# Two graph layers on one core: the last half chunk finished by blocks in PSUM, the first input chunk loaded alone, warming products of a constant zero

## Chip, core and metric

One core of one Trainium2 chip. The metric is the device time of one execution in microseconds (us); of the kernel before it is the median of 3 runs. TensorE is called PE here, VectorE DVE, ScalarE ACT, GpSimd POOL and SyncE SP, as in the profile.

## What is computed

With x (4096 x 128), adj (4096 x 4096) and small weights, all in float32:

```python
u, v = x, v_node_feats
for _ in range(3):
    v = mlp(adj @ u, uv_W1, uv_b1, uv_W2, uv_b2, uv_W3, uv_b3)   # leaky ReLU 0.01 after each layer
    u = mlp(adj @ v, vu_W1, vu_b1, vu_W2, vu_b2, vu_W3, vu_b3)
x = layernorm(x + v)
x = layernorm(x + adj @ (x @ gcn_W))
```

The second u of the last round is not used, so there are six products with adj: five of the rounds and the one of the last line. The kernel takes each product as adj @ (source @ W1): the source is multiplied by the first weight ahead of the product.

## The kernel before

**Tiles and visits.** The 4096 rows of adj are 8 chunks of 512. A tile is 1024 elements in each of 128 partitions: 512 rows of adj by 256 columns. Two tiles make a band, which one DMA of 1 MB loads (L530); `raw_of(t)` is where tile t lies. ACT makes the rounded copy `high` of a tile (`split` on ACT, L571), DVE the rest `low` (`split` on DVE, L728). A visit (`multiply`, L960) is six products of float32r: high with p_low and p_high (four, 512 columns each), then low with p_high (two). All work is put in program order by one counter n: at each n, each engine runs what is due there, and PE then runs visit n of 772. Each tile is split six visits ahead (`AHEAD`). A product's 8 sums are finished, or kept in `part`, and copied back into a PSUM bank by ACT (`seed`) when a later visit goes on with them.

**Start.** SP loads the first weight with x turned, in three pieces of 2, 2 and 4 chunks (`X_PIECES`), then four bands into `early`, then bands into the ring `raw`; a band of the ring is loaded again only after DVE has lowered both tiles that were in it (`load`, wait on `low_ready`). PE begins with 9 products of a zeroed block of `h` (`WARMING`, L975; DVE zeroes it, L724), which fill the time until x is there. Then `project_x` (L893) makes x @ uv_W1 for chunks 0 to 7, ACT raises each (L575) and DVE lowers it (L733). A float32 product of 128 columns is two records in the trace. `X_SPLIT` says before which tile's split a chunk is raised and lowered: chunks 0 to 3 before tile 0, and 4, 5, 6, 7 before tiles 2, 4, 6, 8. Tile t first needs chunk t // 2. The first sum's layer work begins at n = 16: ACT L623 and L624, DVE L754, then PE L866, L867, L869 at n = 19.

**End.** Sums of the last product become `chunks` with a start n: the visit after the sum closes, or 3 after the start before it, whichever is later (`SPACING`). The last row of adj is done apart (`last_sweep`): 12 tiles into a sum that is kept (ACT L589 copies it to `part`), then the 4 last tiles (`IN_HALVES`) are visited for rows 0 to 255 (half 0) and again for rows 256 to 511 (half 1), in products of 256 columns, each half in a bank of its own. For a half DVE adds sum and part (`finish_half`, L749, at the half's start), PE multiplies by gcn_W into `proj` (`project`, L900, start + 2), DVE adds x (L787), takes statistics (L791, L794; `measure`, start + 3), ACT takes the root (L656, start + 4), DVE inverts (L802, L805, start + 5), and ACT (half 0, L663, start + 6) or DVE (half 1, L811) normalizes. SP stores each half (L549). In `measure` of half 0 and `finish_half` of half 1, order on DVE is that of n; at the same n the chunk with the lower number comes first.

```python
HALF_PROJECT, HALF_MEASURE, HALF_ROOT, HALF_INVERT, HALF_NORMALIZE = 2, 3, 4, 5, 6
apart = SPACING[s.product] if s.product == self.sums[self.chunks[-1].total].product else BETWEEN
s.read = max(s.read, self.chunks[-1].start + apart)
```

In the kernel before, half 0 starts at n = 768 and half 1 at n = 772, after the last visit, 771; half 0's `project` is at n = 770 and its `measure` at n = 771.

Of the kernel before, what the change touches and what calls it, by code (L numbers as in the profile page):

```python
# [12 lines left out]
D = 128  # L13
# [23 lines left out]

X_PIECES = [2, 2, 4]

X_SPLIT = [0, 0, 0, 0, 2, 4, 6, 8]  # L40

CONSTS_AT, OTHER_CONSTS_AT, RESIDUAL_AT = 12, 22, 200

WARMING = 9

# [36 lines left out]
HALF = CHUNK // 2  # L82
IN_HALVES = 4
BETWEEN = 14


@dataclass
class Sum:


# [15 lines left out]
    seed: int = -1  # L106
    seeded: int = -1


# [18 lines left out]
class Plan:  # L128
# [100 lines left out]
    def last_sweep(self):  # L229
        rows = list(range(CHUNKS))[::-1]  # L230
        opened = [self.open(LAST, rows[r], "finish") for r in range(1, OPENED + 1)]
        for r in range(1, OPENED + 1):
            self.one(rows[r], self.band(rows[1:r + 1]), opened[r - 1])
        self.one(rows[0], self.band(rows[:1]), self.open(LAST, rows[0], "finish"))
        for r in range(1, OPENED + 1):
            self.one(rows[r], self.band(rows[:1]), opened[r - 1])
            self.one(rows[OPENED + r], self.band(rows[:OPENED + r + 1]), self.open(LAST, rows[OPENED + r], "finish"))
        columns = self.band(rows)
        self.one(rows[-1], columns[:-IN_HALVES], self.open(LAST, rows[-1], "keep"))
# [36 lines left out]
    def place_banks(self):  # L276

        holder = [None] * BANKS
        for i in sorted(range(len(self.sums)), key=lambda i: self.sums[i].opens):
            s = self.sums[i]  # L280
            s.bank = min(range(BANKS), key=lambda b: -1 if holder[b] is None else self.sums[holder[b]].read)
            if holder[s.bank] is not None:
                s.before = holder[s.bank]
                assert self.sums[s.before].read <= s.opens
# [17 lines left out]
def gnn_kernel(nc, adj, x_turned, x_nodes, constants, out):  # L302
# [4 lines left out]
    with ExitStack() as ctx:  # L307
# [58 lines left out]
        consts_set = sem("consts_set")  # L366
        nothing_set = sem("nothing_set")
        table_loaded = sem("table_loaded")
        band_loaded = [sem(f"band_loaded{i}") for i in range(EARLY + RAWS // IN_BAND + LATE)]
        high_ready = sem("high_ready")  # L370
# [6 lines left out]
        total_ready = sem("total_ready")  # L377
        half_ready = sem("half_ready")
        x_projected = sem("x_projected")
        first_raised = sem("first_raised")  # L380
# [133 lines left out]
        def _(sp):  # L514
# [8 lines left out]
            def load(t):  # L523
# [41 lines left out]
        def _(act):  # L565
            def split(t):
                buffer = buffers[t // IN_BAND]
                act.wait_ge(band_loaded[buffer], 16 * (len(loads_into(buffer, t // IN_BAND)) + 1))
                if t >= SLOTS:
# [13 lines left out]
            def keep(s):  # L583
# [74 lines left out]
            def normalize(i):  # L658
                act.wait_ge(shift_ready, i - NORM + 1)
                c = sum_of(i).chunk  # L660
                for j in blocks_in(i):
                    target = block_in(resid[:, blocks_of(c)] if normed(i) else part_of(c), j)
                    done = nc.scalar.activation(target, block_in(h[i % 2], j), ACT.Identity,  # L663
                                                bias=shift[:, j:j + 1], scale=rstd[:, j:j + 1])
# [12 lines left out]
            for n in range(END):  # L677
# [4 lines left out]
                for i, chunk in enumerate(chunks):  # L682
# [40 lines left out]
        def _(dve):  # L723
            nc.vector.memset(h[0][:, 0:D], 0.0).then_inc(nothing_set, 1)  # L724

            def split(t):
# [15 lines left out]
            def finish_half(i):  # L742
# [32 lines left out]
            def measure(i):  # L775
# [10 lines left out]
                columns = columns_in(chunks[i].half)  # L786
                nc.vector.tensor_tensor(h[i % 2][:, columns], source[:, columns],  # L787
                                        resid[:, blocks_of(sum_of(i).chunk)][:, columns], ALU.add).then_inc(x_added, 1)
                dve.wait_ge(x_added, i - NORM + 1)
# [18 lines left out]
            def normalize_half(i):  # L808

                for j in blocks_in(i):  # L810
                    done = nc.vector.tensor_scalar(block_in(part_of(sum_of(i).chunk), j), block_in(h[i % 2], j),  # L811
                                                   moments[:, j, 0:1], rstd[:, j:j + 1], op0=ALU.subtract, op1=ALU.mult)
# [49 lines left out]
        def _(pe):  # L862
# [34 lines left out]
            def turning(i, source, weight):  # L897

                for j in blocks_in(i):
                    done = nc.tensor.matmul(block_in(proj, j), block_in(source, j), weight, start=True,  # L900
# [18 lines left out]
            def project(i):  # L919
                if chunks[i].half < 0:  # L920
                    pe.wait_ge(total_ready, i - FINAL + 1)
                else:
                    pe.wait_ge(half_ready, chunks[i].half + 1)
# [18 lines left out]
            def multiply(n):  # L942
# [16 lines left out]
                def add(p, a, j, first, last):  # L959
                    return nc.tensor.matmul(bank[:, into], p[parity][:, block(j)], a[slot][:, columns(j)],  # L960
                                            start=(first and n == s.opens and s.seed < 0), stop=(last and n == s.closes),
                                            skip_group_check=s.seed >= 0)

# [8 lines left out]

            pe.wait_ge(nothing_set, 1)
            for _ in range(WARMING):
                nc.tensor.matmul(block_in(proj, 0), block_in(h[0], 0), block_in(h[0], 0), start=True, stop=True)  # L975
            for c in range(CHUNKS):
                project_x(c)
            for n in range(END):
                for i, chunk in enumerate(chunks):
                    if layered(i):  # L980
# [4 lines left out]
                        if n == chunk.turn:  # L985
                            turn(i)
                    elif n == place(i, PROJECT, HALF_PROJECT):
                        project(i)
                if n < len(visits):
                    multiply(n)  # L990
# [36 lines left out]
```

## Time and profile before

| | us |
|---|---|
| median of 3 runs (lowest, highest) | 1157.84 (1157.8, 1158.52) |
| the profiled execution's own time | 1157.88 |
| its span, first to last instruction | 1155.9 |
| PE busy | 1149.8 (99%) |
| ACT busy | 726.6 (63%) |
| DVE busy | 721.2 (62%) |
| float32r products L960, of 128x512 | mean 388 to 391 ns each |
| load of 1 MB into `raw`, issue to landing | 5.5 (median) |

The durations of products overlap, since each is pipelined behind the one before: what counts is the distance between their starts. The span leaves out 2.0 us of the profiled execution's time. The granted clock of the profile reads 1.00 of full in all stretches in which PE works.

### The profile page before, as it was taken

How to read it: one execution, taken by the hardware profiler on the slowest of the kernel's cores; microseconds unless marked ns; L12 is line 12 of the kernel's file. 1: busy time of each engine (PE TensorE's matmuls, PEld its weight loads, DVE VectorE, ACT ScalarE, POOL GpSimd, SP SyncE). 2: the span in 40 equal slices, each digit the busy share in tenths (PEclk: the TensorE clock that was granted, in tenths of full speed). 3: DMA queues.
4: the chain of work that ended last, by engine and by line, in shares of the span. 5: the costliest groups of instructions: out<-in, count | busy, mean ns of one | idle time of the engine just before them, and what ended most of it. 6: DMA issues, size and time to landing. Idle time of an engine off the chain costs nothing.

```text
span 1155.9 us, 14073 instructions
## 1 busy us (share of the span) xinstructions
PE 1149.8 (99%) x5314; PEld 961.3 (83%) x5314; DVE 721.2 (62%) x837; ACT 726.6 (63%) x925; POOL 4.2 (0%) x12
## 2 busy tenths in 40 slices
PE   9999999999999999999999999999999999999998
PEld 8888888888888888888888888888888888888887
DVE  6987545554665344765553585545558775459996
ACT  6876654455776444876554486544567874459884
POOL 0000000000000000000000000000000000000000
PEclk9999999999999999999999999999999999999999
DMA  9997656645855576666553584656558565579990
GB/s 384 387 365 274 231 197 244 229 178 195 319 185 207 190 276 234 242 231 255 218 182 145 196 349 182 224 197 234 198 196 327 206 230 191 216 274 371 373 382 22
DMA packets 39361, 281.42 MB, mean 243 GB/s; under 512 B 4416, under 2 KB 4800, under 8 KB 5632
## 3 DMA queue, kind: packets, MB, share of 16 engines
q1 hardware_dynamic: 38736, 278.69, 64.1%
q0 software_dynamic: 560, 1.84, 0.4%
q8 instruction: 44, 0.72, 0.2%
q14 instruction: 21, 0.17, 0.0%
HBM read 278.41 MB, written 2.10 MB: 243 GB/s over the span
## 4 chain that ended last, share of the span: by engine, by line
PE 99%; DVE 0%; issue 0%; ACT 0%; DVEq 0%
PE acc L960 90%; PE proj L900 4%; PE layer L869 1%; PE layer L866 1%; PE layer L867 1%; PE proj L975 0%; PE acc L893 0%; PE proj L893 0%; PE layer L893 0%; DVE stats L791 0%; DVE h L787 0%; DVE h L749 0%; DVE part L811 0%; ACT std L656 0%; DVEq L307 0%
## 5 line engine op out<-in xcount | busy, mean ns | idle before, releaser
L960 PE MATMUL acc<-high,p_low 128*128 128x512 f32 x1544 | 603.0, 391 | 0.0
L960 PE MATMUL acc<-high,p_high 128*128 128x512 f32 x1544 | 598.9, 388 | 0.0
L728 DVE TENSOR_TENSOR low<-raw,high 128x1024 fp32r<-128x1024 f32 x482 | 562.2, 1218 | 47.5 <-ACT high L571 46.8
L571 ACT ACTIVATE high<-raw 128x1024 fp32r<-128x1024 f32 x482 | 485.9, 1054 | 70.9 <-PE acc L960 49.0
L960 PE MATMUL acc<-low,p_high 128*128 128x512 f32 x1544 | 473.8, 388 | 0.0
L960 PEld LDWEIGHTS acc<-low,p_high 128*128 128x128 f32 x1544 | 289.1, 188 | 60.1 <-DVE low L728 0.5
L960 PEld LDWEIGHTS acc<-high,p_high 128*128 128x128 f32 x1544 | 290.1, 188 | 58.1
L960 PEld LDWEIGHTS acc<-high,p_low 128*128 128x128 f32 x1544 | 290.0, 188 | 57.8
L754 DVE TENSOR_TENSOR h_low<-h,h_high 128x512 fp32r<-128x512 f32 x40 | 27.6, 690 | 223.4 <-ACT h L624 223.4
L623 ACT ACTIVATE h_high<-acc,consts 128x512 fp32r<-128x512 f32 x40 | 27.5, 686 | 165.0 <-PE acc L960 165.0
L765 DVE TENSOR_TENSOR p_low<-proj,p_high 128x512 fp32r<-128x512 f32 x32 | 22.1, 690 | 64.1 <-ACT p_high L647 64.1
L759 DVE TENSOR_TENSOR h_low<-h,h_high 128x512 fp32r<-128x512 f32 x32 | 22.1, 692 | 54.1 <-ACT h L632 54.1
L630 ACT ACTIVATE h_high<-layer,consts 128x512 fp32r<-128x512 f32 x32 | 22.1, 689 | 41.6 <-PE layer L869 41.6
L637 ACT ACTIVATE h<-layer,consts 128x512 f32<-128x512 f32 x32 | 22.1, 690 | 40.5 <-PE layer L869 39.6
L647 ACT ACTIVATE p_high<-proj 128x512 fp32r<-128x512 f32 x32 | 19.2, 599 | 41.7 <-PE proj L900 41.7
L728 DVE TENSOR_TENSOR low<-late,high 128x1024 fp32r<-128x1024 f32 x32 | 36.9, 1216 | 0.0
L900 PEld LDWEIGHTS proj<-consts,h 128*128 128x128 f32 x256 | 33.5, 191 | 3.2 <-DVE h L749 0.8
L900 PE MATMUL proj<-consts,h 128*128 128x128 f32 x256 | 33.9, 275 | 0.6 <-DVE h L749 0.6
L632 ACT ACTIVATE h<-layer,consts 128x512 f32<-128x512 f32 x40 | 27.3, 683 | 8.9 <-PE layer L869 8.9
L571 ACT ACTIVATE high<-late 128x1024 fp32r<-128x1024 f32 x32 | 31.9, 1046 | 0.0
L589 ACT ACTIVATE part<-acc 128x512 f32<-128x512 f32 x36 | 21.4, 596 | 12.1 <-PE acc L960 10.9
L624 ACT ACTIVATE h<-acc,consts 128x512 f32<-128x512 f32 x40 | 27.3, 683 | 0.0
(60 smaller groups left out, 333.4 us busy)
## 6 DMA issues: line engine op xcount, KB each, us to landing
raw<-adj_dram SPq DMA_DIRECT2D x241, 1024.0 KB, 5.5
late<-adj_dram SPq DMA_DIRECT2D x16, 1024.0 KB, 7.4
early<-adj_dram SPq DMA_DIRECT2D x4, 1024.0 KB, 11.7
input<-x_dram SPq DMA_DIRECT2D x1, 2048.0 KB, 11.3
out_dram<-part POOLq DMA_DIRECT2D x7, 256.0 KB, 6.5
input<-x_turned_dram SPq DMA_DIRECT2D x1, 1024.0 KB, 6.9
input<-x_turned_dram SPq DMA_DIRECT2D x1, 576.0 KB, 4.1
input<-x_turned_dram SPq DMA_DIRECT2D x1, 512.0 KB, 4.9
```

What stands on the lines that cost most here:

```text
L571: nc.scalar.activation(high[t % SLOTS][:], raw_of(t), ACT.Copy).then_inc(high_ready, 1)
L623: nc.scalar.activation(h_high[:], summed(i)[:], ACT.Prelu, bias=bias, alpha=SLOPE).then_inc(first_raised, 1)
L624: nc.scalar.activation(h[i % 2][:], summed(i)[:], ACT.Prelu, bias=bias, alpha=SLOPE).then_inc(first_ready, 1)
L630: nc.scalar.activation(h_high[:], layer[0][:], ACT.Prelu, bias=bias, alpha=SLOPE).then_inc(second_raised, 1)
L632: nc.scalar.activation(h[i % 2][:], layer[0][:], ACT.Prelu, bias=bias, alpha=SLOPE).then_inc(second_ready, 1)
L637: nc.scalar.activation(h[i % 2][:], layer[1][:], ACT.Prelu, bias=b[f"{way_of(i)}_b3"], alpha=SLOPE).then_inc(third_ready, 1)
L728: nc.vector.tensor_tensor(low[t % SLOTS][:], raw_of(t), high[t % SLOTS][:].bitcast(F32), ALU.subtract).then_inc(low_ready, 1)
L754: nc.vector.tensor_tensor(h_low[:], h[i % 2][:], h_high[:].bitcast(F32), ALU.subtract).then_inc(first_lowered, 1)
L759: nc.vector.tensor_tensor(h_low[:], h[i % 2][:], h_high[:].bitcast(F32), ALU.subtract).then_inc(second_lowered, 1)
L765: nc.vector.tensor_tensor(p_low[k % 2][:, blocks_of(c)], proj[:], p_high[k % 2][:, blocks_of(c)].bitcast(F32), ALU.subtract).then_inc(p_lo ...
L900: done = nc.tensor.matmul(block_in(proj, j), block_in(source, j), weight, start=True, stop=True)
L960: return nc.tensor.matmul(bank[:, into], p[parity][:, block(j)], a[slot][:, columns(j)], start=(first and n == s.opens and s.seed < 0), st ...
```

## The change

At the start, x comes in pieces of 1, 1, 2 and 4 chunks, the first band is loaded by two DMAs of one tile each with a semaphore of its own for the first, the raising of chunks 4 to 7 moves from before tiles 2, 4, 6, 8 to before tiles 5, 7, 9, 11, and the warming products are 8 and read a constant zero that POOL writes before the engines start. At the end, two tiles are visited by halves in place of four. Half 1 goes on in the bank of the kept sum, so that only columns 0 to 255 are kept, and DVE copies its two blocks out one by one. The halves' residual is copied into PSUM by ACT beforehand (`seed_residuals`), block by block into layer[0], layer[0], layer[1] and proj; the products with gcn_W add to it there, and statistics and normalization read PSUM. There are 770 visits then; half 0 closes at n = 767 and starts at 768, half 1 closes at 769 and starts at 771.

```diff
-X_PIECES = [2, 2, 4]
-X_SPLIT = [0, 0, 0, 0, 2, 4, 6, 8]
+X_PIECES = [1, 1, 2, 4]
+X_SPLIT = [0, 0, 0, 0, 5, 7, 9, 11]
-WARMING = 9
+WARMING = 8
-IN_HALVES = 4
+IN_HALVES = 2
...
+            self.sums[total].continues = whole if half else -1
...
+            if s.continues >= 0:
+                s.bank = self.sums[s.continues].bank
...
-                sp.dma_start(band_in(buffer), adj[tiles[t][0], tiles[t][1] // IN_BAND]).then_inc(band_loaded[buffer], 16)
+                band = adj[tiles[t][0], tiles[t][1] // IN_BAND]
+                if t == 0:
+                    sp.dma_start(raw_of(0), band[:, 0:TILE]).then_inc(first_loaded, 16)
+                    sp.dma_start(raw_of(1), band[:, TILE:]).then_inc(band_loaded[buffer], 16)
+                else:
+                    sp.dma_start(band_in(buffer), band).then_inc(band_loaded[buffer], 16)
...
+            def shown(i):
+                if chunks[i].half < 0:
+                    return [h[i % 2]] * IN_CHUNK
+                return [layer[0], layer[0], layer[1], proj]
...
-                nc.scalar.activation(part_of(s.chunk), acc[s.bank][:], ACT.Copy).then_inc(part_kept, 1)
+                columns = columns_in(0 if (s.product, s.chunk) == (LAST, sum_of(len(chunks) - 1).chunk) else -1)
+                nc.scalar.activation(part_of(s.chunk)[:, columns], acc[s.bank][:, columns], ACT.Copy).then_inc(part_kept, 1)
+            def seed_residuals():
+                last = len(chunks) - 1
+                residual = resid[:, blocks_of(sum_of(last).chunk)]
+                act.wait_ge(second_ready, FINAL)
+                act.wait_ge(third_ready, NORM)
+                act.wait_ge(normed_ready, CHUNKS)
+                act.wait_ge(x_added, last - 1 - NORM)
+                nc.scalar.activation(layer[0][:, columns_in(0)], residual[:, columns_in(0)], ACT.Copy).then_inc(residual_seeded, 1)
+                for j in blocks_in(last):
+                    nc.scalar.activation(block_in(shown(last)[j], j), block_in(residual, j), ACT.Copy).then_inc(residual_seeded, 1)
...
+                        if n == chunk.start - 4 and chunk.half == 0:
+                            seed_residuals()
...
-            nc.vector.memset(h[0][:, 0:D], 0.0).then_inc(nothing_set, 1)
...
-                nc.vector.tensor_tensor(h[i % 2][:, columns], acc[s.bank][:, columns], part_of(s.chunk)[:, columns],
-                                        ALU.add).then_inc(half_ready, 1)
+                if s.half == 0:
+                    nc.vector.tensor_tensor(h[i % 2][:, columns], acc[s.bank][:, columns], part_of(s.chunk)[:, columns],
+                                            ALU.add).then_inc(half_ready, 1)
+                else:
+                    for j in blocks_in(i):
+                        nc.vector.tensor_copy(block_in(h[i % 2], j), block_in(acc[s.bank], j)).then_inc(half_ready, 1)
...
+                if chunks[i].half < 0:
+                    nc.vector.tensor_tensor(h[i % 2][:], source[:], resid[:, blocks_of(sum_of(i).chunk)],
+                                            ALU.add).then_inc(x_added, 1)
                 for j in blocks_in(i):
-                    nc.vector.bn_stats(stats[:, j, :], block_in(h[i % 2], j)).then_inc(stats_ready, 1)
+                    if chunks[i].half == 1:
+                        dve.wait_ge(proj_done, i + 1 + blocks_in(i).index(j))
+                    nc.vector.bn_stats(stats[:, j, :], block_in(shown(i)[j], j)).then_inc(stats_ready, 1)
...
+            def project_half(i):
+                half = chunks[i].half
+                pe.wait_ge(residual_seeded, 1 + 2 * half)
+                pe.wait_ge(half_ready, half + 1)
+                for nth, j in enumerate(blocks_in(i)):
+                    if half == 1:
+                        pe.wait_ge(half_ready, half + 1 + nth)
+                    done = nc.tensor.matmul(block_in(shown(i)[j], j), block_in(h[i % 2], j), w["gcn_W"], start=False,
+                                            stop=True, skip_group_check=True)
+                    if half == 1 or nth == 1:
+                        done.then_inc(proj_done, 1)
...
-            pe.wait_ge(nothing_set, 1)
+            zeros = nc.const_aps.tensor(0.0, [D, D], F32)
             for _ in range(WARMING):
-                nc.tensor.matmul(block_in(proj, 0), block_in(h[0], 0), block_in(h[0], 0), start=True, stop=True)
+                nc.tensor.matmul(block_in(proj, 0), zeros, zeros, start=True, stop=True)
```

The normalization of both halves (ACT L663, DVE L811) reads `shown(i)[j]` in place of `h`.

## Rows read from the trace of the kernel before

**Rows 1.** The page: the span, and the shares of the chain that ended last.

```profile
span 1155.9 us, 14073 instructions
...
PE 99%; DVE 0%; issue 0%; ACT 0%; DVEq 0%
```

**Rows 2.** Timeline of the start, 0 to 14: start, duration, engine, line, operation, [idle before].

```profile
0.74 1.33 SPq L517 DMA_DIRECT2D input<-x_turned_dram  x3
...
1.05 4.21 PE L975 MATMUL proj<-h 128*128 128x128 f32 x18 [1.05 <-DVE h L724]
...
5.06 1.78 PE L893 MATMUL proj<-input 128*128 128x128 f32 x8
...
6.68 1.95 PE L893 MATMUL layer<-input 128*128 128x128 f32 x16
...
12.85 0.47 PE L960 MATMUL acc<-high,p_low 128*128 128x512 f32 x1
```

**Rows 3.** DMA issues of the page: KB each, us from issue to landing.

```profile
input<-x_turned_dram SPq DMA_DIRECT2D x1, 1024.0 KB, 6.9
input<-x_turned_dram SPq DMA_DIRECT2D x1, 576.0 KB, 4.1
```

**Rows 4.** Timeline of ACT, 0 to 60: three splits that waited for a band.

```profile
11.02 2.00 ACT L571 ACTIVATE high<-early 128x1024 fp32r<-128x1024 f32 x2 [0.86 <-DMA early<-adj_dram]
...
19.24 2.01 ACT L571 ACTIVATE high<-early 128x1024 fp32r<-128x1024 f32 x2 [0.86 <-DMA early<-adj_dram]
...
35.30 2.01 ACT L571 ACTIVATE high<-raw 128x1024 fp32r<-128x1024 f32 x2 [1.56 <-DMA raw<-adj_dram]
```

**Rows 5.** Timeline of DVE, 10 to 60: splits, lowering of x, lowering of the first layer.

```profile
12.11 2.36 DVE L728 TENSOR_TENSOR low<-early,high 128x1024 fp32r<-128x1024 f32 x2 [1.23 <-ACT high L571]
...
22.99 0.68 DVE L733 TENSOR_TENSOR p_low<-proj,p_high 128x512 fp32r<-128x512 f32 x1
23.59 9.16 DVE L728 TENSOR_TENSOR low<-raw,high 128x1024 fp32r<-128x1024 f32 x8
...
38.49 0.69 DVE L754 TENSOR_TENSOR h_low<-h,h_high 128x512 fp32r<-128x512 f32 x1 [0.88 <-ACT h L624]
```

**Rows 6.** Timeline of PE and its weight loads, 20 to 42: tile 8's low, first layer.

```profile
24.86 0.30 PEld L960 LDWEIGHTS acc<-low,p_high 128*128 128x128 f32 x2 [0.29 <-DVE low L728]
...
39.50 0.39 PE L869 MATMUL layer<-h_low,w_high_uv_W 128*128 128x512 f32 x1
```

**Rows 7.** Timeline of SP, 27 to 29: the load of tiles 18 and 19.

```profile
28.24 0.33 SPq L530 DMA_DIRECT2D raw<-adj_dram  x1
```

**Rows 8.** Timeline of the end, 1140 to 1156, all engines.

```profile
1144.02 0.60 ACT L589 ACTIVATE part<-acc 128x512 f32<-128x512 f32 x1 [2.90 <-PE acc L960]
...
1148.13 0.61 PE L900 MATMUL proj<-consts,h 128*128 128x128 f32 x4
...
1148.49 0.36 PE L960 MATMUL acc<-high,p_low 128*128 128x256 f32 x1
...
1149.23 0.49 DVE L791 BATCH_NORM_STATS2 stats<-h 128x6 f32<-128x128 f32 x2
...
1149.64 0.30 DVE L794 BATCH_NORM_AGGREGATE moments<-stats 128x2 f32<-128x6 f32 x2
...
1149.77 0.40 PE L960 MATMUL acc<-low,p_high 128*128 128x256 f32 x2
...
1150.26 0.42 DVE L749 TENSOR_TENSOR h<-acc,part 128x256 f32<-128x256 f32 x1 [0.32 <-PE acc L960]
...
1150.74 0.71 PE L900 MATMUL proj<-consts,h 128*128 128x128 f32 x4 [0.57 <-DVE h L749]
...
1150.99 0.88 ACT L663 ACTIVATE part<-h,shift,rstd 128x128 f32<-128x128 f32 x2 [0.72 <-DVE shift L805]
...
1151.95 0.49 DVE L791 BATCH_NORM_STATS2 stats<-h 128x6 f32<-128x128 f32 x2
...
1153.22 0.60 DVE L811 TENSOR_SCALAR part<-h,moments,rstd 128x128 f32<-128x128 f32 x2
```

More of the change, by code:

```diff
@@ L107 @@
     seeded: int = -1
+    continues: int = -1
 @dataclass
@@ L238, in last_sweep @@
         columns = self.band(rows)
-        self.one(rows[-1], columns[:-IN_HALVES], self.open(LAST, rows[-1], "keep"))
+        whole = self.open(LAST, rows[-1], "keep")
+        self.one(rows[-1], columns[:-IN_HALVES], whole)
         last = [self.tile(rows[-1], column) for column in columns[-IN_HALVES:]]
@@ L366, in gnn_kernel @@
         consts_set = sem("consts_set")
-        nothing_set = sem("nothing_set")
         table_loaded = sem("table_loaded")
+        first_loaded = sem("first_loaded")
         band_loaded = [sem(f"band_loaded{i}") for i in range(EARLY + RAWS // IN_BAND + LATE)]
@@ L378, in gnn_kernel @@
         half_ready = sem("half_ready")
+        residual_seeded = sem("residual_seeded")
         x_projected = sem("x_projected")
@@ L567, in split @@
                 buffer = buffers[t // IN_BAND]
-                act.wait_ge(band_loaded[buffer], 16 * (len(loads_into(buffer, t // IN_BAND)) + 1))
+                if t == 0:
+                    act.wait_ge(first_loaded, 16)
+                else:
+                    act.wait_ge(band_loaded[buffer], 16 * (len(loads_into(buffer, t // IN_BAND)) + 1))
                 if t >= SLOTS:
@@ L662, in normalize @@
                     target = block_in(resid[:, blocks_of(c)] if normed(i) else part_of(c), j)
-                    done = nc.scalar.activation(target, block_in(h[i % 2], j), ACT.Identity,
+                    done = nc.scalar.activation(target, block_in(shown(i)[j], j), ACT.Identity,
                                                 bias=shift[:, j:j + 1], scale=rstd[:, j:j + 1])
@@ L785, in measure @@
                         dve.wait_ge(std_ready, i - NORM)
[L786 to L789, printed above, removed]
+                if chunks[i].half < 0:
+                    nc.vector.tensor_tensor(h[i % 2][:], source[:], resid[:, blocks_of(sum_of(i).chunk)],
+                                            ALU.add).then_inc(x_added, 1)
+                    dve.wait_ge(x_added, i - NORM + 1)
                 for j in blocks_in(i):
-                    nc.vector.bn_stats(stats[:, j, :], block_in(h[i % 2], j)).then_inc(stats_ready, 1)
+                    if chunks[i].half == 1:
+                        dve.wait_ge(proj_done, i + 1 + blocks_in(i).index(j))
+                    nc.vector.bn_stats(stats[:, j, :], block_in(shown(i)[j], j)).then_inc(stats_ready, 1)
                 for nth, j in enumerate(blocks_in(i)):
@@ L810, in normalize_half @@
                 for j in blocks_in(i):
-                    done = nc.vector.tensor_scalar(block_in(part_of(sum_of(i).chunk), j), block_in(h[i % 2], j),
+                    done = nc.vector.tensor_scalar(block_in(part_of(sum_of(i).chunk), j), block_in(shown(i)[j], j),
                                                    moments[:, j, 0:1], rstd[:, j:j + 1], op0=ALU.subtract, op1=ALU.mult)
@@ L897, in turning @@
             def turning(i, source, weight):
-                for j in blocks_in(i):
+                for j in range(IN_CHUNK):
                     done = nc.tensor.matmul(block_in(proj, j), block_in(source, j), weight, start=True,
@@ L919, in project @@
             def project(i):
[L920 to L923, printed above, removed]
+                pe.wait_ge(total_ready, i - FINAL + 1)
                 if i > FINAL:
@@ L960, in add @@
                     return nc.tensor.matmul(bank[:, into], p[parity][:, block(j)], a[slot][:, columns(j)],
-                                            start=(first and n == s.opens and s.seed < 0), stop=(last and n == s.closes),
-                                            skip_group_check=s.seed >= 0)
+                                            start=(first and n == s.opens and s.seed < 0 and s.continues < 0), stop=(last and n == s.closes),
+                                            skip_group_check=s.seed >= 0 or s.continues >= 0)
                 for j in range(PER_TILE):
@@ L986, in _ @@
                             turn(i)
-                    elif n == place(i, PROJECT, HALF_PROJECT):
+                    elif chunk.half < 0 and n == chunk.start + PROJECT:
                         project(i)
+                    elif chunk.half >= 0 and n == chunk.start + HALF_PROJECT:
+                        project_half(i)
                 if n < len(visits):
```

2 lines of the change are left out of this document (added).

## The prediction

> **What bounds the kernel now.** The page comes first: of the span of 1155.9 us, PE is 99% of the chain that ended last [rows 1]. No other engine can shorten the kernel between the first visit and the last; only what PE does before 12.85 us, waits inside its stream, and what follows its last visit can. The timeline of the start shows PE never idle from 1.05 on: 9 warming products (18 records, 0.22 us each), then the eight projections, then visit 0 at 12.85 [rows 2]. The first 8 records of projection last 0.20 each (5.06 to 6.68), the other 56 take 6.17 us, 0.110 each: the lower level of the clock (1.2 GHz), then the higher one (2.4 GHz) from about 6.5, though the granted clock reads 1.00 throughout. Behind PE, three chains run close: bands landing just in time for ACT [rows 4], DVE without a gap from 12.11 on [rows 5], and one place where PE waited for it, tile 8's `low` at 24.86, 0.29 us [rows 6]. At the end the last visit is used by DVE at 1150.26 and the last normalization ends at 1153.82, so 3.56 us of tail before the store [rows 8].
>
> The profiled execution took 1157.88 us, 0.04 above the median; the sum is made against it. What a measurement of this kernel can tell from no change is about 0.2%, 2.3 us; both ends of this change are smaller.
>
> **Start, warming and projections.** The wait for DVE's zeros goes, so PE can begin where SP does, at about 0.74 in place of 1.05; 16 records at 0.22 end at 4.3. The first piece of x is 320 KB in place of 576. It landed at 0.74 + 4.1 = 4.84; the last piece (1024 KB, issued about 1.6, 6.9 later) landed at 8.5 [rows 3], so 1536 KB took 3.7 us and 256 KB less are worth 0.6: landing at about 4.2. Projections begin at 4.3, not 5.06. If the clock rises at 6.5 as before, 10 records run at 0.22 and 54 at 0.110, and visit 0 comes at 12.45: 0.4 earlier. One SP issue more for x and one more for the band cost 0.4 us each on SP (three took 1.33), but the band behind them lands at 11.02, at the end of a queue that is never empty from the first piece on: nothing.
>
> **Start, the chain behind it.** PE keeps these 0.4 us only if `low` of the next tiles is earlier too. The first half band needs half of the 2.5 us between 8.5 and 11.02: ACT starts at 9.8, DVE lowers tile 0 at 10.9, tile 1 at 12.1 to 13.3. Then tile 2 needs the second band, at the same rate 2.5 after the first, at 13.5, so DVE idles till about 14.5; before, that hole held a chunk of x, which `X_SPLIT` now puts off. The fourth band lands at 19.24 in either kernel (the queue's bytes are the same), so DVE begins tile 6 at 20.3, against 20.7 before (two splits ahead of 22.99). From there DVE is saturated: a split each 1.14 us (9.16 for 8), a lowering of x each 0.61 (22.99 to 23.59) [rows 5]. Before, one lowering was left, and tile 8 was ready at 24.80. Now three are, before tiles 7, 9 and 11: tile 7 is ready at 20.3 + 1.14 + 0.61 + 1.21 = 23.3, tile 9 at 26.15, tile 11 at 20.3 + 5 x 1.14 + 3 x 0.61 + 1.21 = 29.05. Between tile 8's `low` at 24.99 and L869 at 39.50 lie 64 products, 0.227 each, so a visit is 1.36 [rows 6]. PE uses a late tile about 0.2 after it is ready (24.80 to 24.99: the weight load at 24.86 and 0.13 of it) and before it reached tile 11 at 24.99 + 3 x 1.36 = 29.07. Now it reaches it at 29.05 + 0.2 = 29.2. So the 0.4 is eaten at tiles 7, 9 and 11, and the start costs **+0.15**; bounds: -0.4 (the chain is a little faster than this) and +0.3.
>
> The loads of later bands are released by DVE's lowering. That of tiles 18 and 19 was issued at 28.24, behind tile 11 [rows 7]; now at 29.05, 0.8 later. It landed at 35.30, 7.1 us after issue, where the median is 5.5, so 1.5 us were queueing and much of the 0.8 disappears in it. What would be late next is the first layer: ACT's copies queue behind tiles 18 and 19, DVE's L754 ends at 39.18, PE uses it at 39.50 [rows 5, 6], a slack of 0.32. I take the landing as 0.3 later, so **0**; bounds 0 and +0.5 (0.8 less 0.3).
>
> **End, PE.** Two tiles, visited twice in 6 products of 256 columns, are visited once in 6 of 512: 24 records at 0.12 go, 12 at 0.227 come, 0.16 less. Half 0's projection leaves the middle of half 1's visits: between 1148.01, where the last record before it began, and 1148.49 lay 0.48 in place of 0.12 [rows 8]. **-0.52** together, by which the last visit ends earlier.
>
> **End, tail.** Both halves' projections now come after the last visit: half 0's is at n = 770, as far as PE gets when its visits are out. `measure` of half 0 is at n = 771 and so is `finish_half` of half 1, and half 0 has the lower number. DVE therefore waits for half 0's projection and takes its statistics before it copies out half 1. Let A be the moment at which DVE can use the last visit (1150.26 before, 0.37 after its last record began). Half 0's four records begin 0.12 behind that record and last 0.61 [rows 8], so statistics start at A + 0.40. The two aggregates begin 0.41 after that (1149.23 to 1149.64) and last 0.30 together; the next instruction can begin before they end, and I take 0.22 after their start, an estimate between 0.1 and 0.3. The copies start at A + 1.03. A copy of 128 columns: from 0.42 for 256 and 0.69 for 512 (a two-input add, the nearest row), 0.29; bounds 0.2 and 0.35. First copy out at A + 1.32, PE's first product 0.06 later, two records, 0.71 less 0.22 = 0.49: A + 1.87. The second block is 0.2 behind. Statistics, root and inverse follow as before: from the start of the first statistics to the end of normalization 1.87 us were taken (1151.95 to 1153.82, all in instructions that stay). The second statistics now starts at A + 2.1, its place before was 0.2 behind the first, so the end is A + 2.1 - 0.2 + 1.87 = A + 3.77. Half 0's normalization on ACT (0.88) starts after its inverse, at about A + 1.85, and ends at A + 2.75, just where the root of half 1 is wanted; 0.05 for that. A + 3.8 in place of A + 3.56: **+0.24**. In it are the two additions that go: half 0's residual add stood outside, half 1's 0.42 inside. They are seeded by ACT, three copies of at most 0.6 each near 1141, where ACT idled 2.90 [rows 8], and each later wait on them is long over. Half 1's first visit waits for ACT's copy of the kept half; that took 0.60 from 1144.02 and two visits of 0.72 lie between. Without that cover it would cost those 0.6.
>
> The row of L811, 0.60 for two normalizations of 128 columns out of SBUF, is kept for the same out of PSUM: x's lowering with a PSUM input and the first layer's with none take 0.68 and 0.69 [rows 5]. The Trainium skill (VectorE: DVE Perf Modes, "Why PSUM operands drop a tier") says that an operand in PSUM holds a float32 operation to one element a cycle, where one with a single input from SBUF may take two. No row before shows L811 from PSUM; by that rule the two would grow by half of 128 columns at 1.05 ns each, 0.07 apiece, and the sum by 0.13.
>
> **Sum.** 1157.88 + 0.15 + 0 - 0.52 + 0.24 = 1157.75; against the median **1157.7**.
>
> **Rivals.** (1) *The start keeps its gain*: the fourth band lands earlier, or ACT and DVE have slack that this sum does not see. For it: before, tile 6 was only just late. Against: DVE has no idle time in rows 5. Then -0.4 for +0.15: 1157.2. (2) *Slower*: the postponed lowerings delay the loads of tiles 18 to 23 in full, and PE waits at L869. It decides from a landing 0.32 us later than 35.30. Price 0.5: 1158.3, and with tail copies at their upper bound 1158.7. (3) *The clock*: if x's first piece lands late (at 4.8) behind shorter warming, PE idles about 0.5 us before the clock has risen, and the projections stay at the lower level: 54 records at 0.11 more, 5.9 us: 1163.6. Against it: PE was busy from 1.05 and would be but for that half microsecond. The Trainium skill (TensorE: Matmul & The Clock Gate, "What's actually happening") says that the gate's timing is not tied to the kernel's start; no single trace shows that. (4) *The change does not do what it says*: that half 1 is finished block by block can save 0.2 us at most, behind half 0's statistics; this is in the sum and has no chance of its own.
>
> **How the numbers follow.** Forecast 0.55 (own range 1157.3 to 1158.1), rival 1 0.25, rival 2 0.17, rival 3 0.03. 1156.9 to 1158.7 holds the forecast and rivals 1 and 2 with the bounds of the copies (0.2) and most of the spread of runs (0.7). Only rival 3 leaves the 0.2%: slower 0.03; faster 0.01; same 0.96.
>
> **What would show it.** Right: PE's first projection at 4.3, visit 0 at 12.4 to 12.5, new waits of PE's weight loads on DVE at tiles 7, 9 and 11, with tile 11's `low` used at 29.2; at the end four records of projection right behind the last visit, DVE's statistics of half 0 ahead of the copies, and 3.8 us from A to the last normalization. Wrong: visit 12 earlier than before by 0.3 (rival 1); a wait at L869 (rival 2); projection records at 0.22 after 7 us (rival 3); copies ahead of half 0's statistics.

## The result, and the profile after

| | before | after |
|---|---|---|
| median of 22 runs each (lowest, highest), us | 1157.89 (1157.67, 1158.52) | 1159.55 (1158.96, 1160.95) |
| profiled execution, its own time | 1157.88 | 1159.06 |
| its span | 1155.9 | 1157.3 |

The ratio after to before is 1.0015, interval [1.0009, 1.0021]: slower by 1.66 us, where 1157.7 was forecast and 1158.7 was the upper end of the range. It lies inside the 0.2% that the prediction called no change, and outside its range. The times also spread more than before (2.0 us against 0.9). One execution each of e2_band, e4_warm, e5_split, e7_134 and e11_116 below took 1279 to 6156 us; without it the median falls by at most 0.2, and as it was the profiled one of e5_split (6156) and of e7_134 (3052, PE slow throughout), nothing is read from the trace of the first and only the start of its DMA from that of the second.

The profiled execution lies near the fast edge of the 22, so its 1.18 us of difference (1.4 by the spans) shows the pattern and not the whole size.

First the timeline of the start of the changed kernel, to be held against [rows 2] (start, duration, engine, line, operation, [idle before]):

```profile
0.74 1.81 SPq L532 DMA_DIRECT2D input<-x_turned_dram  x4
...
0.78 3.37 PE L1027 MATMUL proj<-const-float32-0.0 128*128 128x128 f32 x16 [0.78 <-PEq L1058]
...
3.99 1.05 PE L935 MATMUL proj<-input 128*128 128x128 f32 x8
...
4.88 1.06 PE L935 MATMUL layer<-input 128*128 128x128 f32 x8
...
7.94 1.13 PE L935 MATMUL layer<-input 128*128 128x128 f32 x8 [2.00 <-DMA input<-x_turned_dram]
...
10.38 2.92 PE L935 MATMUL acc<-input 128*128 128x128 f32 x24 [0.42 <-DMA input<-x_turned_dram]
...
13.95 0.48 PE L1012 MATMUL acc<-high,p_low 128*128 128x512 f32 x1
```

The first projection starts 1.07 us sooner than before, and its records last 0.11 at once: in this execution the clock was at its higher level by 3.99. Then PE stands still for 2.00 us for chunk 2 and 0.42 for chunk 4, and visit 0 begins at 13.95, 1.10 later than before. In the profiled execution before nothing waited for x. Why x is late is in the DMA engines' rate over three stretches (length, granted clock, busy share, GB/s), first of the kernel before, then of the changed one:

```profile
3.00:5.00 2.00, 1.00 1.00 409
5.00:6.50 1.50, 1.00 1.05 442
6.50:8.00 1.50, 1.00 1.00 421
```

```profile
3.00:5.00 2.00, 1.00 1.03 340
5.00:6.50 1.50, 1.00 0.77 178
6.50:8.00 1.50, 1.00 1.04 401
```

From 5.0 to 6.5 the changed kernel moves 178 GB/s in place of 442: 0.27 MB against 0.66. With the 69 GB/s less before, 0.53 MB are missing by 6.5, 1.2 us of DMA at full rate, and all that is queued behind is late by that and more. ACT's splits, to be held against [rows 4], show it:

```profile
11.47 1.06 ACT L594 ACTIVATE high<-early 128x1024 fp32r<-128x1024 f32 x1 [0.88 <-DMA early<-adj_dram]
12.73 1.06 ACT L594 ACTIVATE high<-early 128x1024 fp32r<-128x1024 f32 x1 [0.20 <-DMA early<-adj_dram]
15.26 2.01 ACT L594 ACTIVATE high<-early 128x1024 fp32r<-128x1024 f32 x2 [1.47 <-DMA early<-adj_dram]
...
20.54 1.06 ACT L594 ACTIVATE high<-early 128x1024 fp32r<-128x1024 f32 x1 [0.35 <-DMA early<-adj_dram]
```

The half band that was to land at 9.8 landed at 11.47, the fourth band at 20.54 and not 19.24. Behind that come waits of PE's weight loads for DVE's `low`, five in place of two (before: 0.18 us at 21.99, tile 6, and 0.29 at 24.86, tile 8); three of them:

```profile
17.63 0.30 PEld L1012 LDWEIGHTS acc<-low,p_high 128*128 128x128 f32 x2 [0.20 <-DVE low L764]
...
24.67 0.30 PEld L1012 LDWEIGHTS acc<-low,p_high 128*128 128x128 f32 x2 [0.28 <-DVE low L764]
...
30.40 0.30 PEld L1012 LDWEIGHTS acc<-low,p_high 128*128 128x128 f32 x2 [0.28 <-DVE low L764]
```

They bring the 1.10 to 1.47 (chunk 1's turn into `proj` begins at 74.06, before at 72.59), and that stays until the end. Nothing is added at the first layer: tiles 18 and 19 land 0.97 later than before (35.30), but PE is 1.45 late by then, and its first-layer product L911 comes 1.46 after that of [rows 6]. The issue of that load, its split and the product:

```profile
30.38 0.33 SPq L550 DMA_DIRECT2D raw<-adj_dram  x1
...
36.27 2.01 ACT L594 ACTIVATE high<-raw 128x1024 fp32r<-128x1024 f32 x2 [0.62 <-DMA raw<-adj_dram]
...
40.96 0.39 PE L911 MATMUL layer<-h_low,w_high_uv_W 128*128 128x512 f32 x1
```

The end of the changed kernel, to be held against [rows 8]:

```profile
1150.63 0.40 PE L1012 MATMUL acc<-low,p_high 128*128 128x256 f32 x2
1150.88 0.61 PE L977 MATMUL layer<-consts,h 128*128 128x128 f32 x4
1151.52 0.50 DVE L833 BATCH_NORM_STATS2 stats<-layer 128x6 f32<-128x128 f32 x2 [1.41 <-PE layer L977]
...
1152.16 0.49 DVE L790 COPY h<-acc 128x128 f32<-128x128 f32 x2
...
1152.60 0.46 PE L977 MATMUL layer<-consts,h 128*128 128x128 f32 x2 [1.11 <-DVE h L790]
...
1153.16 0.30 DVE L833 BATCH_NORM_STATS2 stats<-layer 128x6 f32<-128x128 f32 x1 [0.21 <-PE layer L977]
...
1154.44 0.41 DVE L853 TENSOR_SCALAR part<-layer,moments,rstd 128x128 f32<-128x128 f32 x1
1154.77 0.40 DVE L853 TENSOR_SCALAR part<-proj,moments,rstd 128x128 f32<-128x128 f32 x1
```

The last record of the last visit begins at 1150.75, so the visit is usable 0.37 later, at A = 1151.12: 0.86 after the kernel before. Of the 1.47, PE's end has thus won back 0.61. Half 0's four records run right behind, DVE takes half 0's statistics ahead of the copies, and the normalization ends at 1155.17, A + 4.05, against 3.56. The whole end is worth 0.61 - 0.49 = 0.12 us, and 1.47 - 0.12 = 1.35 is about what the two spans differ by.

### The profile page after: what moved, and what is told of

Its sections match the earlier page's. It is cut to its first block, busy times and chain, and to the rows that moved or that the text cites. A ratio compares the mean times of both kernels' runs of the same rounds, so it can differ in the third digit from the quotient of the medians.

```text
span 1157.3 us, 14051 instructions
## 1 busy us (share of the span) xinstructions
PE 1149.0 (99%) x5300; PEld 959.4 (83%) x5300; DVE 720.8 (62%) x835; ACT 726.6 (63%) x928; POOL 4.2 (0%) x12
## 3 DMA queue, kind: packets, MB, share of 16 engines
q0 software_dynamic: 560, 1.84, 0.4%
## 4 chain that ended last, share of the span: by engine, by line
PE 99%; DMA 1%; DVE 0%; SPq 0%; issue 0%; DVEq 0%; ACT 0%
PE acc L1012 90%; PE proj L942 4%; PE layer L911 1%; PE layer L908 1%; PE layer L909 1%; DMA input<-x_turned_dram 1%; PE acc L935 0%; SPq L532 0%; DVE stats L833 0%; PE layer L977 0%; PE proj L935 0%; DVE part L853 0%; DVE moments L836 0%; DVEq L314 0%; ACT std L692 0%
## 5 line engine op out<-in xcount | busy, mean ns | idle before, releaser
L613 ACT ACTIVATE part<-acc 128x512 f32<-128x512 f32 (+1 forms) x36 | 21.2, 590 | 14.2 <-PE acc L1012 13.0
```

## The experiments

Each was timed beside the kernel before, whose median was 1157.89 to 1157.96, in 11 executions (5 of e11_116); a ratio's interval is about 0.0009 to each side (0.0014 for e11_116). Differences below are of medians against the kernel before, in us; with that interval, about 1 us, one alone is weak where it is under 1, and the argument rests on the traces with them. A trace is of one execution, not always one near the median.

**One part at a time.** Four kernels, each the kernel before with one part of the change, or (e3_end) the end alone.

```diff
 e1_pieces
-X_PIECES = [2, 2, 4]
+X_PIECES = [1, 1, 2, 4]
 e2_band
+                if t == 0:
+                    sp.dma_start(raw_of(0), band[:, 0:TILE]).then_inc(first_loaded, 16)
+                    sp.dma_start(raw_of(1), band[:, TILE:]).then_inc(band_loaded[buffer], 16)
 e3_end
 the changed kernel with X_PIECES, X_SPLIT, WARMING, its zeroed block and the first band's load of before
 e4_warm
-WARMING = 9
+WARMING = 8
+            zeros = nc.const_aps.tensor(0.0, [D, D], F32)
```

> Only x in pieces of 1, 1, 2, 4 chunks; all else as before. In the changed kernel the DMA engines moved 156 to 205 GB/s from 5.0 to 6.5 us, where the kernel before had 410 to 467, and everything loaded behind came 1.2 to 1.9 us later. Theory P (the fourth piece of x, with rows of 2.0 to 2.5 KB, makes that slump): the slump is in this trace, x's last piece lands near 10.4 and not 8.5, visit 0 begins at 13.5 or later, and the time is 1158.8 to 1159.8. Theory Q (the two half-band loads make it): no slump, time 1157.5 to 1158.0. Theory W (the warming products of the constant make it): as Q.

> Only the first band in two DMAs of one tile each. Theory P: x lands as before, the first tile's high starts near 11.0 all the same because x's chunks are not raised sooner, or up to 1 us sooner; time 1157.5 to 1158.1. Theory Q: slump of the DMA rate near 5 to 6.5 us and x's last piece 1 to 2 us later; time 1158.8 to 1159.8. Theory W: as P.

> The end of the changed kernel with the start of the kernel before. The two traces give: last visit 0.60 earlier, tail 4.05 in place of 3.56 us, together 0.1 less. If the end is worth what the two traces show: 1157.6 to 1158.0, start as before. If the loss of the changed kernel lay in the end (half 0's statistics ahead of half 1's copies, statistics and normalization out of PSUM): 1158.5 or more.

> Only the warming products: 8 of the constant zero and no wait for DVE. First product at 0.78 in place of 1.05. Theory W: DMA slump at 5 to 6.5 us and a time of 1158.8 or more. Theories P and Q: DMA as before, x's first piece lands at 4.8, and visit 0 begins 0 to 0.4 earlier depending on when the clock rises; time 1157.4 to 1158.1, unless the pause of PE between 4.2 and 4.8 keeps the clock low: then 1159 to 1163.

| | us | against before | ratio, interval |
|---|---|---|---|
| e1_pieces | 1159.32 | +1.43 | 1.0012 [1.0004, 1.0021] |
| e2_band | 1158.67 | +0.78 | 1.0004 [0.9995, 1.0014] |
| e3_end | 1157.95 | +0.06 | 1.0001 [0.9992, 1.0010] |
| e4_warm | 1157.85 | -0.04 | 1.0001 [0.9992, 1.0011] |

The pieces of x alone have the slump. DMA rate of e1_pieces:

```profile
5.00:6.50 1.50, 1.00 0.73 153
```

and from its timeline SP's issue of the four early bands, which took 2.13 us before:

```profile
2.58 2.83 SPq L530 DMA_DIRECT2D early<-adj_dram  x4
```

Theory P held in size and place. The half bands make a smaller slump of their own, later than theory Q said and where they are moved, in e2_band:

```profile
5.00:6.50 1.50, 1.00 1.08 453
...
8.00:10.00 2.00, 1.00 0.87 281
```

Before, the second stretch had 438 GB/s. PE, which begins visit 0 0.83 us earlier in this execution than in that of [rows 2], waits at tiles 2, 4 and 6 and is 0.72 late from there on; the time lies between what P and Q had forecast for it. So both kinds of small transfer cost time, each in its own stretch; W fell (451 GB/s from 5.0 to 6.5 in e4_warm). The end gives next to nothing, as the two traces said (0.12 less in them, 0.06 more by the medians, neither clear of the noise). The profiled execution of e3_end was its slowest (1158.62): in it a later layer's product waited 0.94 us for DVE at 65.77.

**The later raising of x.** e5_split and e12_split are one kernel, timed twice.

```diff
-X_SPLIT = [0, 0, 0, 0, 2, 4, 6, 8]
+X_SPLIT = [0, 0, 0, 0, 5, 7, 9, 11]
```

> Only the raising of x's chunks 4 to 7 moved from before tiles 2, 4, 6, 8 to before tiles 5, 7, 9, 11. My prediction's chain: DVE idles while it waits for the second band and is saturated from tile 6 on, so PE waits for low at tiles 7, 9, 11 and reaches tile 11's low about 0.15 us later: time 1157.9 to 1158.3, with new short waits of PE's weight loads on DVE. If the order does not matter: within 0.1 of before and no new waits. In the changed kernel five such waits sum to 1.3 us, behind late bands.

> The same kernel as e5_split, for a profile of an undisturbed execution. It measured 1158.79 there, 0.83 above before. My prediction's chain gives 0.15 from waits for low at tiles 7, 9, 11; the size of its error should be seen in them, or behind: DVE idle for 1.2 us before tile 2, later loads of bands, a wait at the first layer (L869). If the first layer waits: 0.3 to 0.6 of the 0.83 there.

1158.79 and 1158.78, +0.83 and +0.86, above the 1157.9 to 1158.3 that the prediction's chain gave. From e12_split's timeline, in order of time: waits of PE's weight loads, among them (29.51, SP) the issue of the load of tiles 18 and 19 and (37.14, ACT) their split:

```profile
22.07 0.30 PEld L960 LDWEIGHTS acc<-low,p_high 128*128 128x128 f32 x2 [0.49 <-DVE low L728]
...
23.80 0.30 PEld L960 LDWEIGHTS acc<-low,p_high 128*128 128x128 f32 x2 [0.51 <-DVE low L728]
...
26.67 0.30 PEld L960 LDWEIGHTS acc<-low,p_high 128*128 128x128 f32 x2 [0.26 <-DVE low L728]
...
29.51 0.33 SPq L530 DMA_DIRECT2D raw<-adj_dram  x1
29.54 0.30 PEld L960 LDWEIGHTS acc<-low,p_high 128*128 128x128 f32 x2 [0.29 <-DVE low L728]
...
37.14 2.01 ACT L571 ACTIVATE high<-raw 128x1024 fp32r<-128x1024 f32 x2 [2.24 <-DMA raw<-adj_dram]
...
39.52 0.30 PEld L960 LDWEIGHTS acc<-low,p_high 128*128 128x128 f32 x2 [0.49 <-DVE low L728]
...
41.08 0.19 PEld L869 LDWEIGHTS layer<-h_low,w_high_uv_W 128*128 128x128 f32 x1 [0.81 <-DVE h_low L754]
```

PE waits at tiles 6, 7, 9 and 11, as the chain of the prediction says (and 6 besides: the fourth band landed at 19.70 here). Tile 11's `low` is used at 29.54, 29.2 was forecast. But the band of tiles 18 and 19 is issued at 29.51, 1.27 later than before, and lands 1.84 later: nothing of it disappears in the queue. L869, used at 39.50 before, is used at 41.09. That is rival 2's mechanism. PE is 0.58 later than before when tile 11 is done, 1.70 after tile 18 and L869, 1.86 in the end. This execution took 1159.74, the slowest of its 11; the median has 0.86, so how much of that is the first layer's is not shown.

**What of the pieces stalls the DMA engines.** All with the kernel before, `X_PIECES` alone changed: [2, 2, 2, 2], [1, 3, 4], [1, 1, 6] and [2, 1, 1, 4].

> x in four pieces of two chunks each (rows of 4.5, 4, 4, 4 KB), all else as before. Theory N (the number of DMAs, one more than before, makes the slump of the DMA rate): slump, time 1158.8 to 1159.6. Theory S (small rows, 2.0 and 2.5 KB, make it): no slump, packets of 8 KB keep their 309 ns, time 1157.7 to 1158.1. Theory S' (any change between a stretch of short packets and packets of 8 KB in mid-stream): in between.

> x in three pieces of 1, 3 and 4 chunks (rows of 2.5, 6, 8 KB), as many DMAs as before, first chunk loaded alone. Theory N: no slump, first piece lands near 4.0 and not 4.8, time 1157.5 to 1157.9. Theory S: packets of 8 KB near 5 to 6.5 us take longer than 309 ns, though there is only one small piece; time 1158.2 to 1159.3.

> x in three pieces of 1, 1 and 6 chunks (rows of 2.5, 2 and 12 KB): as many DMAs as before, two small pieces first. Theory S2 (two small pieces at the front make the DMA engines stall some 3 us after their first packet, whatever their number): packets of 8 KB of 0.5 to 1.5 us there, time 1158.8 to 1159.8, and later still since chunks 2 to 7 come together. Theory N2 (it takes a small piece and a fourth DMA together): packets keep 0.31 us; PE waits for the last piece till about 8.5; time 1158.0 to 1158.6.

> x in four pieces of 2, 1, 1 and 4 chunks (rows of 4.5, 2, 2, 8 KB): two small pieces behind a large one. If two small pieces make the stall wherever they stand: packets of 8 KB over 0.5 us some 3 us after the first packet, time 1158.8 to 1159.6. If only at the front, where the engines are still starting (first packets 0.6 to 0.7 us each): packets keep 0.31, time 1157.7 to 1158.2.

Times of the packets that the trace records one by one, begun 2 to 6.5 us after the first one of 2 KB or more (e10_best, below, has the pieces of e7_134 and another end; e13 and e14 are the changed kernel with the pieces, or the first band's load, of before):

```
pieces             median us   against before   packets     count   mean ns   max ns
2, 2, 4 (before)                                8 KB        164     309       312
2, 2, 2, 2         1158.14     +0.18            8 KB         34     309       309
                                                4 KB        383     159       159
1, 3, 4            1157.76     -0.20            8 KB        172     311       392
1, 1, 2, 4 (e1)    1159.32     +1.43            8 KB        110     434      1578
2, 1, 1, 4         1159.13     +1.18            8 KB        136     366      1240
1, 1, 6            1162.75     +4.83            12 KB       109     560      1429
1, 3, 4 (e10)      1156.63     -1.29            8 KB        179     312       453
changed kernel     1159.55     +1.66            8 KB        102     424      2074
2, 2, 4 (e13)      1159.09     +1.14            8 KB        128     309       316
1, 1, 2, 4 (e14)   1159.38     +1.43            8 KB        107     409      2024
```

Theory N falls twice: four DMAs with rows of 4 KB have no slow packet, and three DMAs with two small ones have many (e11_116; its 14 packets of 12 KB begun after 8 us took 467 ns on average). Theory S falls too: one small piece does next to nothing (e7_134). Two do it in both places tried, in front and behind a large piece: with rows of 2.0 to 2.5 KB, packets of 8 KB that are moved after them take up to 2.07 us in place of 0.31. Behind the large piece it is milder (1.24 us at most). Whether the number of small DMAs counts or that of small packets (128 each) is not told apart. In e2_band 150 packets of 4 KB, begun 5.5 to 8 us after the first, took 200 ns on average and 512 at most, where the kernel of four 4-KB pieces has 159. What inside the DMA engines or in the making of descriptors does this is open; SP's issues are longer in every kernel that has it (four bands 2.83, 2.81 and 2.88 us in e1_pieces, e16_2114 and e11_116, 2.13 before and 2.11 in e6_2222), which may be its cause or its effect.

e11_116 (1162.75, above both of its forecasts) is slower than its slump explains: chunks 2 to 7 come in one piece, PE waits 2.84 us for it, and the clock falls. Its granted clock over 10 to 12 us (the second number) is 0.59, over 12 to 14 us 0.55, and 1.00 again over 14 to 16 us:

```profile
10.00:12.00 2.00, 0.59 1.01 426
```

and in its timeline the wait, and 8 records of projection in 1.63 us (0.2 each, the lower level, 1.2 GHz), which at the higher level (2.4 GHz) take 1.06:

```profile
10.76 2.04 PE L893 MATMUL layer<-input 128*128 128x128 f32 x8 [2.84 <-DMA input<-x_turned_dram]
12.59 1.63 PE L893 MATMUL acc<-input 128*128 128x128 f32 x8
```

**One part undone.** The changed kernel with one part as before: e13 `X_PIECES`, e14 the first band's load, e15 `X_SPLIT`.

> The changed kernel with x in its old pieces of 2, 2, 4. If the pieces are the main cause inside the whole change too: 1158.3 to 1158.8, about 1 below the changed kernel. If the costs overlap wholly (the late raising of x and the split band would hold PE just as long): 1159.2 to 1159.6.

> The changed kernel with the first band in one DMA. Alone the split cost 0.8. Overlap: 1159.2 to 1159.6; no overlap: 1158.6 to 1158.9.

> The changed kernel with x's chunks 4 to 7 raised before tiles 2, 4, 6, 8 as before. Alone the move cost 0.8, by waits at tiles 6 to 11, 18 and at the first layer. In the changed kernel PE starts its visits 1.1 later, so those waits have slack: if so, 1159.3 to 1159.7 and fewer waits of PE on DVE; without overlap 1158.6 to 1158.9.

1159.09, 1159.38, 1159.27: 0.46, 0.17 and 0.28 less than the changed kernel, though alone the three cost 1.43, 0.78 and 0.85, 3.1 in sum. No single one carries the loss. Each makes the same resource late, the tiles that PE visits in its first 40 us, and where one is taken out the others hold PE almost as long. In e13_undo_pieces visit 0 began early again (0.63 us before that of [rows 2]), and PE's loads wait 2.3 us for `low`, 0.7 for `high` and 0.5 at the first layer; by 45 us PE is 1.48 behind, where it is 1.47 behind in the changed kernel. Its time lies between its two forecasts, so the costs overlap in part. These differences are small against the spread of these kernels (1.2 us); that they are each less than alone is clear for the pieces only.

**The end, in another order.** e3_end's kernel, half 1 starting at n = 770 in place of 771, so that DVE copies half 1 out ahead of half 0's statistics; and then half 0's inverse and normalization behind half 1's statistics too.

```diff
 e8_order and e9_order2
+                apart = 2 if s.half == 1 else apart
 e9_order2
-HALF_PROJECT, HALF_MEASURE, HALF_ROOT, HALF_INVERT, HALF_NORMALIZE = 2, 3, 4, 5, 6
+HALF_PROJECT, HALF_MEASURE, HALF_ROOT, HALF_INVERT, HALF_NORMALIZE = 2, 3, 4, 6, 7
```

> The changed kernel's end with the start of the kernel before, and half 1 starting one n earlier, so that DVE copies half 1's two blocks out before it takes half 0's statistics, and half 1's products follow half 0's at once. In the changed kernel the copies started 1.04 us after the last visit was usable, 0.6 of that behind half 0's statistics, and the tail was 4.05. If that order is what costs: tail 3.4 to 3.6, time 1157.3 to 1157.5. If the DVE queue only moves the wait (half 0's statistics now stand before half 1's): tail 3.8 to 4.05, time 1157.7 to 1158.0.

> As e8_order, and half 0 inverted and normalized two places later, behind half 1's statistics (HALF_INVERT 6, HALF_NORMALIZE 7). In e8_order half 1's products were done near 1150.5 but its statistics started at 1151.11, behind half 0's inverse, and its root at 1151.93 behind half 0's normalization on ACT; tail 3.82 from 1149.36. If the order of DVE's and ACT's queues is what holds the tail: statistics of half 1 some 0.5 earlier, tail 3.2 to 3.4, time 1156.9 to 1157.2. If the chain of half 1 alone holds it: tail 3.8, time 1157.3 to 1157.6.

e8_order took 1157.42 (-0.54, ratio 0.9995 [0.9986, 1.0004], so not clear of the noise), e9_order2 1156.83 (-1.09, ratio 0.9990 [0.9981, 0.9999]); its slowest execution (1157.32) is faster than the fastest of e3_end (1157.46). The end of e9_order2:

```profile
1149.77 1.15 PE L973 MATMUL layer<-consts,h 128*128 128x128 f32 x6
1150.03 0.49 DVE L786 COPY h<-acc 128x128 f32<-128x128 f32 x2 [1.01 <-PE acc L1008]
1150.43 0.49 DVE L829 BATCH_NORM_STATS2 stats<-layer 128x6 f32<-128x128 f32 x2
...
1151.05 0.28 DVE L829 BATCH_NORM_STATS2 stats<-layer 128x6 f32<-128x128 f32 x1
...
1151.78 0.30 ACT L686 ACTIVATE std<-moments,eps 128x2 f32<-128x2 f32 x1 [0.31 <-DVE moments L832]
...
1152.64 0.40 DVE L849 TENSOR_SCALAR part<-proj,moments,rstd 128x128 f32<-128x128 f32 x1
```

The copies start at A = 1150.03, half 1's first record begins 0.36 us after half 0's last one (1.39 in the changed kernel), and the tail is 3.01, against 3.82 in e8_order (3.4 to 3.6 was forecast) and 4.05 in the changed kernel and in e3_end. The same instructions, in another order, are worth 1.04 us.

**The best version.** e9_order2 with the changed kernel's warming products and x in pieces of 1, 3 and 4; first band whole, `X_SPLIT` as before.

> The end of e9_order2 with the changed kernel's warming products (8 of the constant zero, no wait) and x in pieces of 1, 3 and 4 chunks; first band whole and x's chunks raised where the kernel before raised them. If the start is held by what comes behind PE (bands, ACT, DVE), as my prediction said: first projection near 4.0, waits for low at tiles 0 to 8, time within 0.2 of e9_order2. If PE's head start is kept: 0.3 to 0.6 below e9_order2, 1156.4 to 1156.8.

1156.63 (1156.40 to 1157.51), 1.29 under the kernel before, ratio 0.9990 [0.9981, 0.9998], and 0.2 under e9_order2, which is not clear of the noise. Its visits wait for `low` from the first one on:

```profile
12.93 0.30 PEld L1005 LDWEIGHTS acc<-low,p_high 128*128 128x128 f32 x2 [0.32 <-DVE low L757]
15.79 0.30 PEld L1005 LDWEIGHTS acc<-low,p_high 128*128 128x128 f32 x2 [0.28 <-DVE low L757]
```

Visit 0 begins at 11.86, 1.0 before that of [rows 2], in part because the clock rose early in this execution, and by the medians 0.2 us of it is left. The start is held by what comes behind PE.

## Why the prediction was wrong, point by point

**The step that failed** stands in its passages on the start: "One SP issue more for x and one more for the band cost 0.4 us each on SP [...]: nothing", and with it "the fourth band lands at 19.24 in either kernel (the queue's bytes are the same)". The DMA rate was taken as a constant, 1 MB in 2.5 us whatever the rows. The bytes were the same, but the engines lost 0.53 MB by 6.5 us. Two small pieces cost 1.4 us alone, the halved band 0.8, where each had stood at 0. In the sum it is the term +0.15: visit 0 came at 13.95 and not at 12.45, and with the waits behind it the start cost 1.47 in the profiled execution. What the small transfers do to the engines is shown by the packets; why they do it stays open.

**The first layer**: "I take the landing as 0.3 later, so 0". In the changed kernel the 0 came out, but partly by luck. The load was issued 2.14 later (30.38) and landed 0.97 later, not 0.3; PE did not wait because it was itself 1.45 late. Where the later raising stands alone (e12_split) the step fails: issued 1.27 later, landed 1.84 later. What the queue would absorb had been worked out from one landing (7.1 against a median of 5.5); measured, it took in 1.2 of 2.1 us in one kernel and nothing in the other. There the mechanism was rival 2's, with its place (L869) and its point (0.32 late); it was given 0.17, and the changed kernel's profiled execution does not show it.

**Warming and the first projection** came right: first product at 0.78 (0.74), last warming record over near 4.1 (4.3), projection at 3.99 (4.3), and the trade of a warming product for the missing wait costs nothing (e4_warm, -0.04). The clock rose at different moments in different executions: in the profiled ones the first projection runs at the higher level in the changed kernel and at the lower one before. Rival 3 did not happen with this change; what it costs is seen in e11_116.

**The chain behind it**: the prediction saw one wait of PE before, at tile 8; the trace has a second, 0.18 us at tile 6 (21.99). PE's waits at tiles 7, 9 and 11 came in the kernel that has only this move (29.54 against 29.2 for tile 11), with waits of 0.49 to 0.51 at tiles 6 and 7 that were not forecast in that size, and the gain of PE's early start was indeed eaten. With late bands they moved elsewhere in the changed kernel.

**The end, PE**: -0.52 was forecast, 0.61 is what the trace gives. **The end, tail**: the order of DVE's queue was read rightly. Statistics of half 0 at A + 0.40 (forecast 0.40), copies at A + 1.04 (1.03), first product at A + 1.48 (1.38), half 1's first statistics at A + 2.04 (1.9). The end came at A + 4.05, not 3.8. Of the 0.25, 0.10 is the copy and its start (the first block took 0.44 from its start to PE's product, where 0.35 was put), and 0.13 the normalization: 0.41 and 0.40 for a block from PSUM in place of 0.34, 0.73 for both in place of 0.60. The Trainium skill's rule (VectorE: DVE Perf Modes, "Why PSUM operands drop a tier") was put aside for the rows of two-input operations, which cannot show it. The trace agrees with the rule, and with the 0.13 that was worked out from it: a one-input float32 operation out of SBUF had something to lose.

**The sum**: -0.28 for the end became -0.12, +0.15 for the start became 1.47 in the profiled execution and, by the medians, 1.6 (with e3_end's end) to 1.8 (with 0.12 for the end).

## What to carry to other kernels

A transfer cut in small pieces for an earlier first byte has a price at the queue as a whole: look at the GB/s of the next few us, not at the landing of the first piece. One small piece was free here, a second one was not. A change that was worked out for PE alone has to be followed to the loads that it postpones: the later raising of x cost 0.85 alone where 0.15 stood in the sum. Where the last work is a short chain over three engines, write down the order in each engine's queue instruction by instruction before cutting it finer: here the order was worth 1 us and the cutting 0.1.

## What was not expected of the hardware

- Packets of 8 KB that follow 256 packets of 2.0 to 2.5 KB took up to 1.58 us (e1_pieces) and 2.07 us (changed kernel) in place of 0.31, and the engines' rate over 1.5 us was 153 and 178 GB/s in place of 442. 383 packets of 4 KB in a row did not do it.
- After PE had waited 2.84 us for data, its granted clock was 0.59 on average over the next 2 us, and products ran at the lower level, 1.2 GHz (0.2 per record), even after 12.6 us (e11_116). A wait of 2.00 us (changed kernel) left it at the higher level, 2.4 GHz. Each is one execution.
- Costs of three start-up changes that each were 0.8 to 1.4 us alone came to 1.7 together; undoing one gave back 0.2 to 0.5.
